# An attention kernel whose beats run exp scores before maxima scores

## What is computed

```python
x_norm = modulate(_ln(x), shift_a, scale_a)
q, k, v = split(x_norm @ W_qkv + b_qkv)                 # 16 heads of 8
attn_w = softmax(einsum('bhqd,bhkd->bhqk', q, k) * scale)
x = x + gate_a[:, None] * (einsum('bhqk,bhkd->bhqd', attn_w, v) @ W_proj + b_proj)
q_c = _ln(x) @ W_qc + b_qc
k_c, v_c = split(_ln(context) @ W_kvc + b_kvc)          # 77 keys
c_attn_w = softmax(einsum('bhqd,bhsd->bhqs', q_c, k_c) * scale)
x = x + einsum('bhqs,bhsd->bhqd', c_attn_w, v_c) @ W_cproj + b_cproj
x = x + gate_m[:, None] * (gelu(modulate(_ln(x), shift_m, scale_m) @ W_mlp1 + b_mlp1) @ W_mlp2 + b_mlp2)
```

## Time and profile before

| what | value |
|---|---|
| median of three runs | 425.43 us (421.11 to 426.66) |
| the profiled execution | 425.98 us |
| its span, first to last instruction | 424.2 us |
| mean granted clock of PE | 0.95 |
| length of a slot in the middle | 17.0 us |

### The profile page before, as it was taken

One profiled execution on the slowest core, in us unless ns is written; L12 is line 12 of the kernel. 1 busy time (PEld: TensorE's weight loads), 2 busy tenths in 40 slices (PEclk: granted clock), 3 DMA queues, 4 the chain that ended last, 5 costly groups with the idle time before them and its releaser, 6 DMA issues.

```text
span 424.2 us, 14629 instructions
## 1 busy us (share of the span) xinstructions
PE 360.5 (85%) x5186; PEld 248.5 (59%) x5186; DVE 266.8 (63%) x684; ACT 273.8 (65%) x531; POOL 195.5 (46%) x455
## 2 busy tenths in 40 slices
PE   2768777698898899999999999898897497999995
PEld 2657564465666667667676676675665354445442
DVE  5454445777887878879788788796754450433411
ACT  1334455477777778787778787877783448567672
POOL 2813027656575575766756757565461410111200
PEclk9977698989999999999999999999996978999999
DMA  6250506433333433344234433343311300000101
GB/s 163 69 140 14 143 3 172 110 88 95 78 92 92 103 99 77 89 102 112 76 88 104 109 77 89 96 103 97 78 44 39 76 4 2 24 26 26 49 25 49
DMA packets 65520, 33.10 MB, mean 78 GB/s; under 512 B 8332, under 2 KB 65228, under 8 KB 65484
## 3 DMA queue, kind: packets, MB, share of 16 engines
q1 hardware_dynamic: 62732, 31.77, 29.2%
q10 hardware_dynamic: 2752, 0.86, 0.9%
HBM read 4.83 MB, written 2.10 MB: 16 GB/s over the span
## 4 chain that ended last, share of the span: by engine, by line
PE 40%; issue 20%; DVE 13%; SPq 8%; POOL 6%; DMA 5%; ACT 3%; ACTq 3%; DVEq 1%; POOLq 0%
PE wide L1123 7%; PE ps_o L1131 6%; SPq L394 6%; PE ps_misc L1159 4%; PE wide L1061 4%; PE ps_o L1083 4%; DMA qkc_st<-qkcp 3%; DVE mx L673 2%; DMA qk_st<-qkp 2%; PE wide L1097 2%; SPq L399 2%; POOL qkp L485 2%; POOL qkp L487 2%; PE wide L1072 2%; PE ps_misc L1172 2%
## 5 line engine op out<-in xcount | busy, mean ns | idle before, releaser
L673 DVE TENSOR_REDUCE mx<-wide 128x8 f32<-128x1024 f32 x64 | 77.9, 1218 | 23.6 <-PE wide L1061 23.5
L853 ACT ACTIVATE p_c<-wide 128x1024 f32<-128x1024 f32 x64 | 65.8, 1029 | 32.0 <-PE wide L1072 32.0
L853 ACT ACTIVATE p_s<-wide 128x1024 f32<-128x1024 f32 x64 | 65.5, 1023 | 20.4 <-PE wide L1072 19.4
L673 DVE TENSOR_REDUCE mxc<-wide 128x8 f32<-128x616 f32 x64 | 50.5, 789 | 21.5 <-PE wide L1061 21.5
L1083 PE MATMUL ps_o<-p_c,vc_m 128*32 128x128 f32 x1024 | 43.4, 290 | 0.8 <-ACT p_c L853 0.6
L1083 PE MATMUL ps_o<-p_s,v_m 128*32 128x128 f32 x1024 | 43.4, 290 | 0.0
L1061 PE MATMUL wide<-qk_st 62*128 62x128 bf16 x512 | 26.7, 226 | 11.6 <-DVE mx L673 7.8
L1061 PE MATMUL wide<-qkc_st 62*128 62x77 bf16 x512 | 21.1, 207 | 13.7 <-DMA qkc_st<-qkcp 7.9
L1123 PE MATMUL wide<-m_nT,w_sb 128*128 128x512 f32 x64 | 30.7, 616 | 0.2 <-DVE mxc L673 0.2
L649 DVE TENSOR_SCALAR x_n<-xs,x_mv,x_rstd 128x128 f32 (+1 forms) x64 | 20.8, 367 | 15.4 <-POOL x_rstd L480 15.4
L1061 PEld LDWEIGHTS wide<-qk_st 62*128 62x128 bf16 x512 | 15.3, 97 | 25.7 <-DVE mx L673 12.3
(11 more groups left out here) (147 smaller groups left out, 824.6 us busy)
## 6 DMA issues: line engine op xcount, KB each, us to landing
qk_st<-qkp SPq DMA_DIRECT2D x96, 128.0 KB, 2.5
qkc_st<-qkcp SPq DMA_DIRECT2D x96, 128.0 KB, 2.5
xs<-x SPq DMA_DIRECT2D x4, 512.0 KB, 4.6
out<-m_out SPq DMA_DIRECT2D x8, 256.0 KB, 2.3
ctx_sb<-ctx SPq DMA_DIRECT2D x4, 308.0 KB
qk_st<-nmT SPq DMA_DIRECT2D x64, 4.0 KB
qkc_st<-nmcT SPq DMA_DIRECT2D x64, 4.0 KB
w_sb<-L_xcond_W_mlp ACTq DMA_DIRECT2D x2, 256.0 KB, 3.1
```

What stands on the lines that cost most here:

```text
L673: nc.vector.reduce_max(mxt[:, b].rearrange("q (x r) -> q r x", r=2)[:, r], src, AX.X, negate=True).then_inc(sems[done], 1)
L853: nc.scalar.activation(dst[u % 2][:].rearrange("k x q -> k (x q)"), ps_st[:].rearrange("k s x -> k (s x)"), ACT.Exp, scale=SCALE).then_inc ...
```

## The change

On PE, in each beat, the blocks of self and cross maxima scores are moved behind the blocks of self and cross exp scores. The values stay behind both. The waits of each block move with it. No other engine's program changes.

```diff
                 for t in range(BEATS):
-                    use = s.unit(self_max(t))
-                    if use:
-                        p, u = use
-                        ring_free(s, MAX_RING, "self", u, max_read)
-                        if u == 0:
-                            w(pe, f"qk_in{p.par}", 16 * NCMB * (p.turn + 1))
-                        scores(p, u, qk_st, T, "smax_ps")
-                    use = s.unit(cross_max(t))
-                    if use:
-                        p, u = use
-                        ring_free(s, MAX_RING, "cross", u, max_read)
-                        if u == 0:
-                            w(pe, f"qkc_in{p.par}", 16 * NCMB * (p.turn + 1))
-                        scores(p, u, qkc_st, S, "smaxc_ps")
                     use = s.unit(self_exp(t))
                     if use:
                         p, u = use
...
                             w(pe, f"mc_in{p.par}{u // 2}", 16 * 2 * (p.turn + 1))
                         scores_t(p, u, qkc_st, "stc_ps")
 
+                    use = s.unit(self_max(t))
+                    if use:
+                        p, u = use
+                        ring_free(s, MAX_RING, "self", u, max_read)
+                        if u == 0:
+                            w(pe, f"qk_in{p.par}", 16 * NCMB * (p.turn + 1))
+                        scores(p, u, qk_st, T, "smax_ps")
+                    use = s.unit(cross_max(t))
+                    if use:
+                        p, u = use
+                        ring_free(s, MAX_RING, "cross", u, max_read)
+                        if u == 0:
+                            w(pe, f"qkc_in{p.par}", 16 * NCMB * (p.turn + 1))
+                        scores(p, u, qkc_st, S, "smaxc_ps")
                     use = s.unit(self_pv(t))
```

## The result

| | before | after |
|---|---|---|
| median | 424.8 us (4 runs, 421.11 to 426.66) | 430.31 us (4 runs, 428.64 to 433.21) |
| ratio | | 1.0143, 95% interval 1.0098 to 1.0188 |
| profiled execution, its span | 425.98, 424.2 us | 429.09, 427.3 us |
| mean granted clock in the profile | 0.950 | 0.954 |
| slot in the middle (slot 7 to slot 12) | 17.00 us | 17.54 us |

The kernel became slower by 1.4%, some 6 us, which stays inside the forecast range but is twice the forecast amount. The two profiled executions lie 3.1 us apart. Every ratio in this document leaves out executions that took over 1.5% longer than the fastest of the same kernel.

A forecast was written before the change was run, and what follows sets the result against it. No engine was saturated; a chain across engines bounds the loop, with maxima scores straight behind PE jobs in beats 0 and 4. 0.43 + 1.92 + 2.16 - 1.75 = +2.8 us gave 428.2 us, range 423 to 435.

The forecast's parts named there:

- The loop passes M in beats 0 and 4 only: Only in beats 0 and 4 do maxima scores start straight behind PE's earlier jobs, with no exp scores ahead.
- M: The eight maxima score matmuls of a beat on PE (L1061), moved later by the change.
- One M pays 0.24: In beats 0 and 4 the maxima scores start 0.24 us later, the pipelined price; range 0 to 0.39.
- E: The eight exp score matmuls of a beat on PE (L1072), moved ahead of the maxima scores.
- Beat 1 has cover: In beat 1 exp scores hardly wait and the maxima are late by 0 to 0.1 us more, taken as 0.
- Beats 2, 5 and 6 cost and give nothing: PE's gap before maxima scores (beats 2, 6) or 0.8 us of cover (beat 5) hides the exp scores; costed at nothing.
- DVE is busy from mx to s_o, so it is late by just what M lost: In beat 0 DVE runs without a break from mx to s_o, so s_o loses the same 0.24 us.
- The count: Payments by slot: beat 0 pays 0.43 and 8 x 0.24, beat 4 9 x 0.24, less refunds 1.75: +2.8 us.
- Refunds of 1.75: Where maxima scores wait for a transfer, exp scores hide in it: slots 1, 16, 17 at 0.43, 3 and 15 at 0.23.
- A: Rival: a transfer, not PE, sets the maxima scores in beats 0 and 4; nothing is paid, 423.6 us; chance 0.14.
- C: Rival: ACT's head start in beats 2 and 6 shortens the loop, 420.1 us, or 417.3 with nothing paid; chance 0.08.
- B: Rival: exp scores not ready in beat 1 hold maxima scores and values, 438.2 us; chance 0.18 with milder forms.

The follow-up runs named there:

- the wait: Full change, plus POOL's cast of the rest of q_c in beat 0 waiting for DVE's two x_n: slot 17.44 us, ratio 1.0011, again 1.0026.
- the kernel made of refunds alone: Kernel before, with exp scores first only in six places where maxima scores wait for a transfer: slot 17.00 us, ratio 1.0001.

## Why the prediction was right or wrong

- *The loop passes M in beats 0 and 4 only.* Right. The two beats bear all of the growth of the full change, and they add (17.30, 17.23, 17.53). The other six alone cost 0.13, 0.09 of it by the collision.
- *One M pays 0.24.* Right: 0.24 and 0.23, and 0.21 and 0.23 for one more. The whole E of 0.39 would have been wrong.
- *Beat 1 has cover.* Right. E starts at 215.49 and M at 215.73, with no idle time of PE before E; mx of beat 1 comes 2.09 us after that of beat 0, against 2.00 before, but by x_n and not by E.
- *Beats 2, 5 and 6 cost and give nothing.* Right: E twice in beats 2 and 6 left the slot at 17.54, and PE waits for POOL's nmc as before.
- *DVE is busy from mx to s_o, so it is late by just what M lost.* Here the step failed. That a late DVE meets POOL at another point was not in the sum. The pair of x_n rose from 0.61 to 0.70 in slot 10, and the term is 0.10 us a slot (17.54 to 17.44 with the wait). The rows for it were in the trace of before: the cast of 0.50 us beside x_n in slot 11, the pair of 0.78 us in slot 13, and the pair of 1.22 us in slot 4. The predicted slot of 17.4 to 17.5 came out at 17.54.
- *The count.* Mis-sized. By the q_c job of slot 12 after is 265.77 - 260.77 = 5.0 us behind. The sum had 3.4 by there: 0.43, 7 x 0.24 for beat 0 and 8 x 0.24 for beat 4, less two of the refunds, 0.43 and 0.23. Of the 1.6 us between them 1.25 were there by the end of slot 3, where after was 1.0 behind (106.35 against 105.33) and the sum had it 0.2 ahead. The clocks of the two executions differ there, 0.88 and then 0.96 in before between 69 and 87 and 87 and 106 us, 1.00 and then 0.91 in after, so this part can't be put down to the change. Slots 4 to 7 grew by 1.28 us against 1.20 in the sum, and slots 8 to 12 by 2.70 against 2.40: that is the collision's 0.10 a slot less the 0.03 left open above.
- *Refunds of 1.75.* Not shown. From slot 12 to 16 the distance stays at 5.0 to 5.5 us but for 4.76 at slot 14, and the kernel made of refunds alone ties with before.
- *The total.* 428.2 forecast, 430.31 measured. By the sum of the slots the change costs 5 us, and the ratio says 4.2 to 8.0. The profiled execution shows 3.1 because it made up about 2 us behind slot 16 (92.6 us from the q_c job to the end of the span, before 94.7), with a clock of 1.00 instead of 0.91 between 350 and 370 us (it had 0.75 instead of 0.83 between 330 and 350). Its other runs took 431.54 and 433.21 at a mean clock of 0.937, and 428.64 at 0.954. So a profile's total was the wrong thing to hold the sum against; the slots were the right one.
- *Rivals.* A and C were refuted. B's place, beat 1, stayed covered; what was slower than forecast had another cause, which no rival named.

## What to carry to other kernels

Find the operations that start straight behind another engine's jobs in the chain, and put nothing ahead of them; ahead of one that waits for a slower engine, work is free up to the length of that wait (here 0.6 us of matmuls in beats 2 and 6). When an edit shifts one of DVE and POOL against the other, look for what newly overlaps: the 0.24 us of delay in beat 0 brought 0.1 us more with it, and about 0.2 us on top of that brought another 0.5. A wait that makes the uncritical engine come second cost nothing here (17.00 and 17.01) and took this away.

## What the runs showed of the hardware

- A pair of DVE tensor_scalar operations of 128x128 f32 takes 0.59 to 0.61 us by itself, 0.67 to 0.78 where a POOL cast holds the second, and 1.13 to 1.22 with a cast and a subtraction of POOL beside it. Where the first x_n ends 0.01 us ahead of the cast's start, the cast is the longer one (0.50 against 0.40); where it ends 0.04 behind, the pair is (0.78 against 0.59).
- Two groups of eight matmuls of 128 columns on row halves follow each other after 0.21 to 0.24 us, whichever of the two comes first.
- The mean granted clock of the kernel before ran from 0.939 to 0.965 over its executions, and 0.01 goes with 1.8 to 3.5 us of its time, more than the whole effect of some edits here.
